# Taylor attention and routed experts on one core: fillers moved between gaps, two block sums left to the denominator matmuls, queries dealt in 64s

## What is computed

```python
q, k, v = (x @ Wq.T, x @ Wk.T, x @ Wv.T)             # heads: 16 x 16, 16 x 16, 16 x 64
k_enc, v_enc = (x[:, :128] @ Wk_enc.T, x[:, :128] @ Wv_enc.T)
f(x) = concat([1, x / 2, (x outer x) / (4 * sqrt(2))])  # per head
A = tril(f(q) @ f(k).T);  A2 = f(q) @ f(k_enc).T
z = 1 / ((f(q) * (f(k_enc).sum + cumsum(f(k)))).sum(-1) + EPS)
out = ((A @ v + A2 @ v_enc) * z) @ Wout.T
x = layernorm(x + out)
probs = softmax(x @ wr + br); top 2; the first expert's gelu MLP, gated
x = layernorm(x + that)
```

## Time and profile before

| | us |
|---|---|
| median of 3 runs | 1182.94 |
| lowest, highest | 1181.48, 1186.81 |
| the profiled execution | 1180.28 |
| its span, first to last instruction | 1178.5 |
| attention within it | about 48 to 763 |

### The profile page before, as it was taken

One profiled execution on the slowest core, in us unless ns is written; L12 is line 12 of the kernel. 1 busy time (PEld: TensorE's weight loads), 2 busy tenths in 40 slices (PEclk: granted clock), 3 DMA queues, 4 the chain that ended last, 5 costly groups with the idle time before them and its releaser, 6 DMA issues. The chain is left out here.

```text
span 1178.5 us, 16833 instructions
## 1 busy us (share of the span) xinstructions
PE 1063.4 (90%) x5296; PEld 621.4 (53%) x5297; DVE 634.1 (54%) x963; ACT 508.0 (43%) x891; POOL 613.0 (52%) x635
## 2 busy tenths in 40 slices
PE   5699899989989989989999998883679999999994
PEld 4344355445445445436545544463357766766763
DVE  5396864683693683585476468447123343333332
ACT  2466644654654663653664464400123233233231
POOL 1397654664673674665576567500134544444442
PEclk9799989999999999999999998995789999999998
DMA  5733631741651552453273261104821011101010
GB/s 208 260 102 106 201 125 64 234 151 41 201 178 69 176 176 97 141 181 126 70 217 122 84 208 59 36 1 197 349 116 33 29 31 34 33 29 33 30 30 1
DMA packets 54111, 134.91 MB, mean 114 GB/s; under 512 B 5854, under 2 KB 10176, under 8 KB 51746
## 3 DMA queue, kind: packets, MB, share of 16 engines
q1 hardware_dynamic: 50306, 124.81, 31.5%
q0 software_dynamic: 3744, 9.31, 2.5%
HBM read 87.73 MB, written 47.29 MB: 115 GB/s over the span
## 5 line engine op out<-in xcount | busy, mean ns | idle before, releaser
L384 ACT ACTIVATE w<-slot 128x1024 f32<-128x1024 f32 (+1 forms) x256 | 231.2, 916 | 176.3 <-PE slot L730 176.1
L751 PE MATMUL osum<-w,values 128*64 128x512 f32 (+3 forms) x1280 | 253.6, 492 | 5.7 <-DVE w L511 5.7
L508 DVE SCALAR_TENSOR_TENSOR w<-w,mask 128x256 f32<-128x256 f32 (+1 forms) x192 | 175.8, 916 | 150.8 <-ACT w L384 138.0
L343 POOL TENSOR_TENSOR wsum<-w 128x512 f32<-128x512 f32 x64 | 95.7, 1496 | 222.7 <-DVE w L511 222.7
L511 DVE TENSOR_SCALAR w<-w 128x768 f32<-128x768 f32 (+2 forms) x192 | 189.4, 986 | 0.0
L347 POOL TENSOR_TENSOR wsum<-wsum,w 128x768 f32<-128x768 f32 x64 | 124.8, 1951 | 60.0 <-DVE w L511 58.2
L1161 ACT ACTIVATE active<-upT,b 128x128 f32<-128x128 f32 x312 | 84.9, 383 | 158.3 <-PE upT L1239 158.3
L1215 PE MATMUL down<-w,active 128*128 x624 | 144.1, 385 | 2.5 <-ACT active L1161 2.5
L1227 PE MATMUL up<-w,rowsT 128*128 x312 | 143.1, 602 | 0.7 <-ACT rowsT L1150 0.7
L730 PE MATMUL slot<-qop,kop 64*128 64x512 f32 (+3 forms) x640 | 126.6, 426 | 9.8 <-issue 7.2
L1215 PEld LDWEIGHTS down<-w,active 128*128 128x128 f32 x624 | 117.5, 193 | 18.6 <-issue 3.8
(11 more groups left out here) (187 smaller groups left out, 1210.7 us busy)
## 6 DMA issues: line engine op xcount, KB each, us to landing
kop<-k_rows SPq DMA_DIRECT2D x32, 640.0 KB, 5.8
qop<-q_rows SPq DMA_DIRECT2D x32, 512.0 KB, 7.5
w<-in_w SPq DMA_DIRECT2D x16, 1024.0 KB, 9.3
inv<-inv_rows SPq DMA_DIRECT2D x56, 256.0 KB, 4.5
k_rows<-kh SPq DMA_DIRECT2D x32, 320.0 KB
k_rows<-kl SPq DMA_DIRECT2D x32, 320.0 KB
q_rows<-qh SPq DMA_DIRECT2D x32, 256.0 KB
q_rows<-ql SPq DMA_DIRECT2D x32, 256.0 KB
```

The lines of the kernel that those rows point to most:

```text
L343: pool.tensor_tensor(dst[:, 0, :], src[:, 0, 0:N], src[:, 0, N:2 * N], ALU.add)
L384: act.activation(w[:, n % 2, :, at:at + cols], slot[u % 2][:, :, 0:cols], ACT.Square, bias=HALF_ROOT).then_inc(squared, 1)
L508: dve.scalar_tensor_tensor(src[:, :, 0:cut], src[:, :, 0:cut], 0.5, mask[:, 0:cut].unsqueeze(1).to_broadcast([P, 2, cut]), ALU.add, ALU.mu ...
L751: last = pe.matmul(osum[n % 2][HD * s:HD * s + HD, q0:N], values[:, j, h * HD:h * HD + HD], w[:, n % 2, s, at:at + N - q0], start=(u == 0) ...
```

## The change

- Placement: most fillers move one gap later, the query and key projections 3 and 4 two gaps. The turns and the router of batch b - 1 leave gaps 26, 28 and 30 of batch b and come in gaps 7, 9 and 10 of batch b + 1 (function `turned_at`); in the last batch those of batch 5 come at 7, 9, 10 and those of batch 6 at 26, 28, 30. Normalising, moments, deviation and centring move by up to one gap. The attention ring `ATT` has 13 buffers in place of 14.
- SP: the load of y for batch b - 1 moves from the end of a batch's queue to ahead of gather 3 of the next.
- POOL adds three blocks only (encoder, block 0 and block 1: lines 343, 344, 347). The instructions of lines 350 and 354 go. PE takes the unsummed blocks 2 (256 queries) and 3 (128 queries) from `w` itself: eight more matmuls of 128 and 64 columns per pair, in the program 12 in place of 4, each of which is two instructions in the trace.
- Queries dealt in 64s: column group c no longer holds queries 256 c to 256 c + 255 but every second run of 64, so that the short blocks fall into both groups alike. The stores of the inverse, and the spreading in the last batch, follow this order.
- ACT's `square` waits for the denominator matmuls of pair n - 2, in place of `weighed` and POOL's sums.

```diff
--- before.py
+++ after.py
@@ -35,17 +35,25 @@
 UNIT_BLOCKS = [[(NT, 0, 0)], [(0, 0, 0)], [(3, 384, 0), (1, 128, 128)], [(2, 256, 0)]]
 UNIT_AT, UNIT_COLS = [0, 512, 1024, 1536], [512, 512, 512, 256]
 FIXED, FIXES = [0, 2, 4, 6], 6
-RING, ATT, INV = 4, 14, 4
-V_LATE_AT = {0: 0, 1: 1, 3: 2, 5: 3, 6: 4}
-QK_AT = {10: 0, 12: 1, 14: 2, 25: 3, 27: 4}
-OUT_AT = {15: 0, 17: 1, 19: 2, 21: 3}
-V_EARLY_AT = {16: 0, 18: 1, 20: 2, 22: 3, 24: 4}
-TURN_AT, ROUTER_AT = {26: 0, 28: 1}, 30
+RING, ATT, INV = 4, 13, 4
+V_LATE_AT = {0: 0, 1: 1, 3: 2, 4: 3, 6: 4}
+QK_AT = {11: 0, 13: 1, 15: 2, 27: 3, 29: 4}
+OUT_AT = {16: 0, 18: 1, 20: 2, 22: 3}
+V_EARLY_AT = {17: 0, 19: 1, 21: 2, 23: 3, 25: 4}
 XH_GAP, XL_GAP = 7, 8
-NORM_AT = {4: 0, 5: 1, 6: 2, 7: 3, 9: 4, 10: 5, 12: 6, 13: 7}
-INVERT_GAP, MOMENTS_GAP, CENTRE_GAP, RSTD_GAP = 1, 22, 24, 23
+NORM_AT = {4: 0, 5: 1, 6: 2, 7: 3, 9: 4, 10: 5, 11: 6, 13: 7}
+INVERT_GAP, MOMENTS_GAP, CENTRE_GAP, RSTD_GAP = 1, 23, 25, 24
 COPY_UNIT, DEN_UNIT = 0, 3
 QH = N // 2
+
+
+def turned_at(b, g):
+
+    if b >= 2 and g in (7, 9, 10):
+        return [(b - 2,) + {7: ("turn", 0), 9: ("turn", 1), 10: ("router", 0)}[g]]
+    if b == B - 1 and g in (26, 28, 30):
+        return [(b - 1,) + {26: ("turn", 0), 28: ("turn", 1), 30: ("router", 0)}[g]]
+    return []
 
 
 def piece_numbers():
@@ -61,10 +69,7 @@
                 order.append((b - 1, "out", OUT_AT[g]))
             if g in V_EARLY_AT and b + 1 < B:
                 order.append((b + 1, "v", V_EARLY_AT[g]))
-            if g in TURN_AT and b > 0:
-                order.append((b - 1, "turn", TURN_AT[g]))
-            if g == ROUTER_AT and b > 0:
-                order.append((b - 1, "router", 0))
+            order += turned_at(b, g)
     order += [(B - 1, "turn", k) for k in range(2)] + [(B - 1, "router", 0)]
     return {key: n for n, key in enumerate(order)}
 
@@ -239,8 +244,8 @@
                 for s in range(2):
                     for c in range(2):
                         at = 32 * (2 * s + c)
-                        sp.dma_start(inv_rows[PAIRS * s:PAIRS * s + PAIRS, QH * c:QH * c + QH],
-                                     den_sb[at:at + PAIRS, :]).then_inc(inv_out, 16)
+                        rows = inv_rows[PAIRS * s:PAIRS * s + PAIRS, :].rearrange("h (t c n) -> h t c n", c=2, n=64)
+                        sp.dma_start(rows[:, :, c, :], den_sb[at:at + PAIRS, :]).then_inc(inv_out, 16)
 
             def load_inverse(b, g):
                 n = b * PAIRS // 2 + g
@@ -283,6 +288,8 @@
                 if b > 0:
                     for g in range(2, PAIRS // 2):
                         load_inverse(b - 1, g)
+                if b > 1:
+                    load_rows(b - 1)
                 gather(b, 3)
                 if b + 1 < B:
                     send(b + 1, 0)
@@ -292,8 +299,7 @@
                 if b + 1 < B:
                     send(b + 1, 1)
                     gather(b + 1, 1)
-                if b > 0:
-                    load_rows(b)
+            load_rows(B - 1)
             store_rows(B - 1)
             sp.wait_ge(y_stored, 16 * B)
 
@@ -343,15 +349,8 @@
                     pool.tensor_tensor(dst[:, 0, :], src[:, 0, 0:N], src[:, 0, N:2 * N], ALU.add)
                     pool.tensor_tensor(dst[:, 1, :], src[:, 1, 0:N], src[:, 1, N:2 * N], ALU.add).then_inc(wsummed, 1)
                 elif u == 2:
-                    pool.wait_ge(wsummed, 4 * n + 1)
+                    pool.wait_ge(wsummed, 2 * n + 1)
                     pool.tensor_tensor(dst[:, :, P:N], dst[:, :, P:N], src[:, :, 2 * N + P:3 * N],
-                                       ALU.add).then_inc(wsummed, 1)
-                    pool.wait_ge(wsummed, 4 * n + 2)
-                    pool.tensor_tensor(dst[:, :, 3 * P:N], dst[:, :, 3 * P:N], src[:, :, 2 * N:2 * N + P],
-                                       ALU.add).then_inc(wsummed, 1)
-                else:
-                    pool.wait_ge(wsummed, 4 * n + 3)
-                    pool.tensor_tensor(dst[:, :, 2 * P:N], dst[:, :, 2 * P:N], src[:, :, 3 * N:WIDTH],
                                        ALU.add).then_inc(wsummed, 1)
 
             def deviation(b):
@@ -362,12 +361,12 @@
                 pool.tensor_tensor(rstd[:, :], rstd[:, :], minus_half[:, :].to_broadcast([P, NT]),
                                    ALU.pow).then_inc(rstd_step, 1)
 
-            for u in range(1, UNITS):
+            for u in range(1, 3):
                 add_blocks(0, u)
             for b in range(B):
                 for g in range(GAPS):
                     n, u = b * PAIRS + g // UNITS + 1, g % UNITS
-                    if n < B * PAIRS and u > 0:
+                    if n < B * PAIRS and u in (1, 2):
                         add_blocks(n, u)
                     if b > 0 and g == RSTD_GAP:
                         deviation(b - 1)
@@ -379,8 +378,7 @@
                 at, cols = UNIT_AT[u], UNIT_COLS[u]
                 act.wait_ge(scored, UNITS * n + u + 1)
                 if n >= 2:
-                    act.wait_ge(weighed, UNITS * (n - 2) + u + 1)
-                    act.wait_ge(wsummed, 4 * (n - 1))
+                    act.wait_ge(den_full, n - 1)
                 act.activation(w[:, n % 2, :, at:at + cols], slot[u % 2][:, :, 0:cols], ACT.Square,
                                bias=HALF_ROOT).then_inc(squared, 1)
 
@@ -454,8 +452,9 @@
                         high_qk(b + 1, QK_AT[g - 1])
                     if b + 1 < B and g - 1 in V_EARLY_AT:
                         copy_values(b + 1, 0, V_EARLY_AT[g - 1])
-                    if b > 0 and g - 1 in TURN_AT:
-                        copy_turned(b - 1, TURN_AT[g - 1])
+                    for owner, kind, k in turned_at(b, g - 1):
+                        if kind == "turn":
+                            copy_turned(owner, k)
                     if b + 1 < B and g == XH_GAP:
                         split_x_high(b + 1)
                     if b * PAIRS + p + 1 < B * PAIRS:
@@ -592,8 +591,9 @@
                         low_qk(b + 1, QK_AT[g - 1])
                     if b > 0 and g - 1 in OUT_AT:
                         residual(b - 1, OUT_AT[g - 1])
-                    if b > 0 and g - 1 == ROUTER_AT:
-                        logits_of(b - 1)
+                    for owner, kind, _ in turned_at(b, g - 1):
+                        if kind == "router":
+                            logits_of(owner)
                     if n < B * PAIRS and u > 0:
                         finish_weights(n, u)
                     if b + 1 < B and g == XL_GAP:
@@ -682,7 +682,8 @@
                 if p >= 2:
                     pe.wait_ge(normalised, (B - 1) * PAIRS + p - 1)
                 for c in range(2):
-                    last = pe.matmul(spread_bank[p % 2][:, QH * c:QH * c + QH], of_group[:, c, :],
+                    cols = spread_bank[p % 2][:, :].rearrange("p (t c n) -> p t c n", c=2, n=64)[:, :, c, :]
+                    last = pe.matmul(cols, of_group[:, c, :],
                                      inv[:, p // 2, QH * (p % 2):QH * (p % 2) + QH], start=True, stop=True)
                 last.then_inc(spread, 1)
 
@@ -755,15 +756,19 @@
 
             def denominators(n):
                 b, p = n // PAIRS, n % PAIRS
-                pe.wait_ge(wsummed, 4 * n + 4)
+                pe.wait_ge(wsummed, 2 * n + 2)
                 if p == 0 and b > 0:
                     pe.wait_ge(den_copied, b)
-                for s in range(2):
-                    for c in range(2):
-                        at = 32 * (2 * s + c)
-                        last = pe.matmul(den[at:at + 32, 0:QH], onehot[:, 31 - p:63 - p],
-                                         wsum[:, n % 2, s, QH * c:QH * c + QH], start=(p == 0),
-                                         stop=(p == PAIRS - 1), tile_position=(0, at), skip_group_check=True)
+                summands = [(0, lambda s: wsum[:, n % 2, s, :]), (2, lambda s: w[:, n % 2, s, 3 * N:WIDTH]),
+                            (3, lambda s: w[:, n % 2, s, 2 * N:2 * N + P])]
+                for k, (t0, src) in enumerate(summands):
+                    for s in range(2):
+                        for c in range(2):
+                            at = 32 * (2 * s + c)
+                            last = pe.matmul(den[at:at + 32, 64 * t0:QH], onehot[:, 31 - p:63 - p],
+                                             src(s).rearrange("p (t c n) -> p t c n", c=2, n=64)[:, :, c, :],
+                                             start=(p == 0 and k == 0), stop=(p == PAIRS - 1 and k == 2),
+                                             tile_position=(0, at), skip_group_check=True)
                 last.then_inc(den_full, 1)
 
             for i in range(5):
@@ -789,10 +794,11 @@
                         output(b - 1, OUT_AT[g])
                     if b + 1 < B and g in V_EARLY_AT:
                         project_values(b + 1, 0, V_EARLY_AT[g])
-                    if b > 0 and g in TURN_AT:
-                        turn_rows(b - 1, TURN_AT[g])
```

(7 more changed lines are left out.)

## The result

The changed kernel takes 1195.08 us as a median of four runs (1194.73 to 1204.3), the kernel before 1182.21 beside it: a ratio of 1.0125 [1.0081, 1.017]. Run again it gave 1199.23 and 1.0128 [1.0091, 1.0165]. So it is slower by about 15 us by the two ratios (13 and 18 us by the medians). The forecast was +30: right in direction, twice too large. The profiled execution of after has a span of 1202.5 us, 24.0 above the 1178.5 of before. Of these, 23.2 lie in attention, whose last denominator set starts at 786.03 us in place of 762.85.

What follows compares the result with a forecast made beforehand. The prediction took TensorE (PE) as the bound in attention. Its terms, 21.8 + 12.4 + 3.0 - 4.9 = +32.3 us on the profiled 1180.3, gave 1212.6, stated as 1212 us; range 1182 to 1232.

Steps and rivals of the forecast that it cites:

- denominator sets: On PE in attention: 128 and 64 added columns per group cost 0.34 us per pair, 64 pairs, +21.8 us.
- gather wait at gap 4: PE's scores at gap 4 wait for the operand gather, 2.6 us in batch 1, 1.7 in six others; +12.4 us.
- xl, logits, ql waits: PE's waits on VectorE: 22.3 us of new waits replace 19.3 of xl, +3.0; the present ql waits, 2.6, go.
- weight waits: PE's two waits for weights in the last batch, 2.3 us, go because moved turns and router fill PE.
- lower clock: Clock lost on PE behind waits stays the same overall: 0, with 5 us either way.
- the rival of 1262: Denominator sets bound by issuing, or short-set groups not overlapping: 73 us in place of 21.8, about 1262; chance 0.06.
- The logits wait: QK projection 0 in gap 11 waits for VectorE to read the logits, 3.4 us in batches 2 to 6: 17.0.
- Every instruction added to it counts in full: In attention TensorE is the bound, so time comes off only where PE waits and added PE work lengthens the kernel.
- The inverse rows: Stores of the inverse in 128 pieces of 256 bytes cost 0, bounded by 10 us in six VectorE waits.
- rival 2: At gap 4 the gather is late, but VectorE is not: 1187 us; chance 0.17.
- Rival 4: Waits at two places bring the lower clock, or 256-byte rows do their worst: 10 to 15 more, 1225; chance 0.16.
- Rival 1: New placement empties PE's waits, given early gather landing and logits read in time: about 1164 us; chance 0.09.

Runs made afterwards that it cites:

- after_gf: The changed kernel with gather 1 of the next batch ahead of the eight writes of its second send in SP's queue; 1185.28 us, ratio 1.0018.
- place_only: The changed kernel with the denominators of the kernel before (five GpSimd additions, one 256-column set), new placement kept; 1216.99 us, ratio 1.029.
- den_halves: den_only with queries dealt in halves of 256 in place of 64s; 1182.32 us, ratio 1.0008.
- den_only: The kernel before with only the denominators' part of the change (three GpSimd blocks, 24 matmuls, 64s, ACT's wait); 1173.27 us, ratio 0.9922.
- gf_router8: The changed kernel with gather 1 ahead of the second send, and turns and router in gaps 5, 7 and 8; 1167.53 us, ratio 0.9875.
- den_router29: den_only with the router in gap 29 in place of 30, away from the denominator set; 1172.94 us, ratio 0.9927.

## Why the prediction was right in direction and wrong in size

In the profiled executions, which are what the sum was made for:

| term | forecast | measured |
|---|---|---|
| denominator sets | +21.8 | +21.1 |
| gather wait at gap 4 | +12.4 | +18.1 |
| xl, logits, ql waits | +3.0 and -2.6 | -14.8 |
| weight waits | -2.3 | -5.7 |
| kl waits | 0 | -2.6 |
| y wait of the last batch's turn | 0 | +1.5 |
| waits for GpSimd's sums | 0 | -0.9 |
| lower clock | 0, 5 either way | +8.6 |
| sum | +32.3 | +25.3, the span +24.0 |

The prediction's last step has a slip: 32.3 us on the median of 1182.9 are 1215, and on the profiled execution 1212.6; it named the second number for the median.

The waits are those of the list of waits; by starts the idle time is 1.9 us lower still, which gives the 23.4 of the table above.

**The set** (right): 0.90 us against 0.91, and with it the rival of 1262 fell. The Trainium skill (TensorEngine Tiling (Array Packing), Instruction Overhead) puts about 60 cycles on a short matmul, which by the prediction's estimate would have made the change some 6 us longer; the measured set of 0.90 us does not show it.

**The gather** (mechanism right, term too small): from projection 3's end to gap 4 PE needs 18.7 us (forecast 18.8), and the wait came in all seven batches. The landing came 21.1 to 21.8 us after the projection in most (22.5 in batch 2, 19.9 in batch 7), where 20.9 to 21.4 was put. The mean wait is 2.64 us, not 1.83. after_gf shows the queue order as its cause: the wait went with it.

**The logits wait** (failed): forecast 3.4 us in five batches, measured 1.3 and 0.9 in two. Two parts of the step missed. First, VectorE read the logits 12.6 us after its first normalise in batches 2 and 4, not 15.1; in batches 3, 5 and 6 it was 14.7 to 15.1, as forecast. Batch 3 has the same order of work as batch 4 above. VectorE's timeline there, and GpSimd's addition beside it:

```profile
343.96 1.75 DVE L507 SCALAR_TENSOR_TENSOR w<-w,mask 128x512 f32<-128x512 f32 x1
345.64 1.49 DVE L510 TENSOR_SCALAR w<-w 128x512 f32<-128x512 f32 x1
343.52 1.65 POOL L349 TENSOR_TENSOR wsum<-w 128x512 f32<-128x512 f32 x1 [3.11 <-DVE w L510]
```

In both batches the addition starts 0.44 us before the mask. In batch 3 VectorE is the one that is held (1.75 and 1.49 us); in batch 4 GpSimd is (3.20 in place of 1.65), and VectorE takes 0.68 and 0.41. That is the whole 2.15 us between 14.74 and 12.59. Why one gives way and not the other is not shown. Second, PE arrived later than its 18.7 us after gap 4: 20.9, 20.2, 18.7, 22.5 and 22.6 in batches 2 to 6. Behind the gather's wait it ran at the lower clock in batches 2, 3, 5 and 6, and in 5 and 6 once more behind the router. There the set, 0.90 us in batch 4, takes 1.66 (540.13 to 541.79 in PE's timeline of batch 5):

```profile
536.79 1.95 PE L718 MATMUL piece<-wr,yT 128*128 128x8 f32 x16
...
540.13 1.08 PE L768 MATMUL den<-wsum,onehot 128*32 128x256 f32 x8
540.99 0.87 PE L768 MATMUL den<-w,onehot 128*32 128x128 f32 x16
541.79 0.94 PE L627 MATMUL piece<-xh,wqk_h 128*128 128x512 f32 x2
```

With 18.7 in every batch the logits, as late as they were, would have cost about 11.4 us in five waits (an estimate from these starts). So of the 14.8 us that are missing from the 17.0, about 5.6 are VectorE's and 9.2 are PE's own lateness, which the sum holds as clock loss. The clock term that was put at 0 and this wait replace each other; together they are 10.8 us where 17.0 stood. In batches 5 and 6 the logits were read 22.0 and 22.2 us after the wait at gap 4 ended, where 22.1 was forecast. In place_only, with five additions, they were read later still, 23.2 to 23.8 us after it, and PE waited 17.8 us in five waits.

The term of 0 for the clock also rested on a reading that was too kind to before. The prediction has the batches behind batch 1 at 0.98 to 1.00, but batch 5 (496.39 to 591.43) took 95.04 us at 0.96.

**"Every instruction added to it counts in full"** (failed): this sentence of the first part is the fault in the reasoning. It holds only where PE's idle time is used up, as in den_halves. PE had 39.7 us of idle time in attention, nearly all behind VectorE, and the same part of the change that adds 21.1 us to PE takes from VectorE what makes PE wait. The durations were forecast well (xl 1.07 us shorter), but their value was counted only for xl and for the way to the logits. VectorE's relief was put at 1.5 us over eight gaps, which is what the way from the first to the sixth normalise shows (15.75 to 14.15 in den_only); over a whole batch VectorE is busy for 4.4 us less (57.4 to 53.0), and only part of that was counted. By medians the denominators' part is worth -8 us in the old placement, -22 in the new one (1216.99 to 1195.08), -11 there with the gather ahead (1196.17 to 1185.28) and -27 with both edits; in none of the four is it a cost. That the total came out as a loss is all placement, +35 us with the old denominators and +22 with the new.

**The inverse rows** in pieces of 256 bytes (right): the first normalise follows the scores that the landing released by 6.6 to 7.0 us in batches 1 to 6 and by 6.1 in batch 7. In place_only, with pieces of 1 KB in the same placement, it is 6.6 to 7.2 and 5.7. The Trainium skill (DMA: Bandwidth & Descriptors, Specifications) puts line rate at 512 bytes and above; no cost of the smaller pieces shows in these times. VectorE's wait for inv averages 9.1 us (63.9 in seven) as forecast "5 or above".

**The rivals.** The time fell between rival 2 (gather late, VectorE not, 1187) and the forecast. Rival 2 is nearer in what happened: the gather was late and VectorE was early in two batches of five. Rival 4, the lower clock, came too, with 8.6 of its 10 to 15 us. Rival 1 was to decide at a landing 2 us earlier; after_gf, in which no gather wait is left, shows that this alone doesn't do it (1185.3), and gf_router8, in which the logits wait is gone too, comes near its 1164 with 1167.5.

**What stays open.** The sum of the terms closes on the profiled execution, +25.3 against +24.0, but the other executions of after lie 4 to 16 us below the profiled one of their series (1204.3 and 1208.2), while for before the profiled one lies 2.7 below the median. In den_only the profile accounts for 3 of the 8 to 9 us: its profiled execution (1177.12) lies 3.9 above its median. The profiled executions had granted clocks of 0.943 and 0.939 and the fastest timed one, 1191.94, had 0.955. That points to the clock term, but no trace was taken of a timed execution, so which of its stretches are shorter isn't shown. The measured +15 is therefore explained only as far as the profile goes.

## What to carry to other kernels

A busy share of 90% doesn't make an engine the bound: split its idle time by who ends it, and if a change adds work to it and relieves the engine it waits for, both count, and the sign is open until the waits are added up. Two waits in a row that hang on the same chain stand in for each other, so removing one shows little (10 and 0 us here) and removing both shows all (28). When a producer of a transfer is moved later in a queue, count the other transfers that stand between it and its gather, here eight writes and some 21 us.

## What the runs showed of the hardware that was not expected

- Where VectorE and GpSimd work side by side, either can give way, even with the same 0.44 us between their starts. At 432.42 of after VectorE's masking took 1.77 us while GpSimd's addition took 1.66; at 441.45 the same instruction took 0.68 while the addition beside it took 3.20.
- The clock fell behind 16 router matmuls of 8 columns and a set with 16 short ones, in which PE was busy throughout (0.99, then 0.50, in den_only). It cost a batch about 1.5 us there, against 3.4 in the two batches of after shown above. In den_only such a stretch stands at five of the six ends of batches 1 to 6. In den_halves, whose batches leave PE idle for 0.4 us, it stands at all six. In before, with the same router in the same gap and no short matmuls in the set, it stands at none. In den_router29, with the router a gap away from the set, it stands at two.
- The set of 24 matmuls and 24 weight loads in four column groups took 0.90 us, 19 ns an instruction. The 36 ns of the set before, which the prediction took as the upper end (its 73 us), was no limit of issuing.
